# One wide transpose for the maxima, one norm for two at the input, wider cleans, range clears and new priorities in a planned transformer kernel

## What is computed

```python
x = x + LN(L0_attn(LN(x)))   # own input norm with gain and shift, plus positions; 6 layers of
                             # windowed attention (16 heads of 8, past 125 keys, one zero row ahead)
                             # and a GELU feed-forward of 512, post-norm
x = x + LN(L0_ffn(LN(x)))    # token shift, sigmoid gate times squared relu
x = x + LN(L1_attn(LN(x)))   # causal attention with a phase gate for each head and key
x = x + LN(L1_ffn(LN(x)))    # a router picks 3 of 8 experts for each sequence
```

## Time and profile before

| what | value |
|---|---|
| median of 3 runs | 1100.56 us (1100.5 to 1101.69) |
| span of the profiled execution, first to last instruction | 1102.7 us |
| TensorE busy (matmuls) | 994.2 us, 90% of the span |
| VectorE, ScalarE, GpSimd busy | 809.7, 763.1, 407.5 us |
| mean granted TensorE clock | 0.972 of full |

### The profile page before, as it was taken

The page is one execution under the profiler, slowest core; times in us unless marked ns, Lnnn a source line. Parts: engine busy times, 40 slices in busy tenths (PEclk is TensorE's granted clock), DMA queues, the critical chain, the costliest instruction groups (busy, mean ns, idle before and its releaser), DMA issues.

```text
span 1102.7 us, 47422 instructions
## 1 busy us (share of the span) xinstructions
PE 994.2 (90%) x20080; PEld 705.4 (64%) x20080; DVE 809.7 (73%) x2451; ACT 763.1 (69%) x1418; POOL 407.5 (37%) x544
## 2 busy tenths in 40 slices
PE   1679999999999999999998999998987988899993
PEld 0356777777777777777775777666664544555772
DVE  6777887777778887777777775879798979872320
ACT  7457666767777667767773777767767868688741
POOL 8711433333344433333344213444646353401311
PEclk9769999999999999999998999999999989999997
DMA  5522211222225211332224123221112020401220
GB/s 160 116 62 61 61 42 42 78 70 61 62 62 105 56 43 41 64 89 62 61 62 103 27 38 61 60 46 29 35 28 60 3 61 4 117 26 37 68 77 10
DMA packets 72627, 64.80 MB, mean 59 GB/s; under 512 B 16226, under 2 KB 66914, under 8 KB 72418
## 3 DMA queue, kind: packets, MB, share of 16 engines
q1 hardware_dynamic: 72418, 61.78, 23.3%
HBM read 15.70 MB, written 1.05 MB: 15 GB/s over the span
## 4 chain that ended last, share of the span: by engine, by line
PE 72%; DVE 11%; ACT 5%; POOL 5%; issue 3%; SPq 1%; DMA 1%; POOLq 0%; DVEq 0%; ACTq 0%
PE b L775 11%; PE b L887 9%; PE b L878 8%; PE b L676 7%; PE b L756 5%; PE b L790 4%; PE b L959 4%; PE b L949 4%; PE b L709 4%; PE b L806 2%; PE b L846 2%; PE b L871 2%; DVE mx L1218 2%; ACT probs L1021 2%; PE b L862 2%
## 5 line engine op out<-in xcount | busy, mean ns | idle before, releaser
L1021 ACT ACTIVATE probs<-b 128x443 f32<-128x443 f32 (+2 forms) x736 | 354.0, 543 | 137.5 <-PE b L756 96.5
L1218 DVE TENSOR_REDUCE mx<-b 128x2 f32<-128x378 f32 (+1 forms) x768 | 353.0, 508 | 93.9 <-PE b L709 93.5
L676 PE MATMUL b<-band,identb 64*64 64x252 bf16 x2304 | 170.4, 286 | 18.4 <-DVE mx L1218 8.1
L775 PE MATMUL b<-probs,vals 128*32 128x189 f32 (+5 forms) x3968 | 182.8, 311 | 1.2 <-DVE mx L1218 0.3
L775 PEld LDWEIGHTS b<-probs,vals 128*32 128x32 f32 x3968 | 115.1, 110 | 47.2 <-issue 12.2
L1543 POOL TENSOR_SCALAR veps<-mv 128x4 f32<-128x4 f32 x48 | 11.0, 230 | 352.4 <-DVE mv L1324 352.4
L756 PE MATMUL b<-qpack,kpack 64*64 64x189 bf16 (+5 forms) x3968 | 137.0, 236 | 0.3 <-issue 0.3
L709 PE MATMUL b<-kpack,qpack 62*64 62x189 bf16 (+1 forms) x3072 | 122.0, 239 | 1.0 <-issue 1.0
L676 PEld LDWEIGHTS b<-band,identb 64*64 64x64 bf16 x2304 | 67.0, 105 | 83.6 <-issue 36.5
L887 PE MATMUL b<-w,hid 128*128 128x128 f32 x768 | 110.1, 287 | 0.0
L1215 DVE TENSOR_REDUCE mx<-b 128x1 f32<-128x512 f32 (+7 forms) x256 | 99.3, 444 | 14.1 <-PE b L724 13.7
(11 more groups left out here) (173 smaller groups left out, 1695.7 us busy)
## 6 DMA issues: line engine op xcount, KB each, us to landing
kpack<-kparts SPq DMA_DIRECT2D x168, 128.2 KB
qpack<-qparts SPq DMA_DIRECT2D x168, 128.0 KB, 3.4
qpack<-mrows SPq DMA_DIRECT2D x224, 4.0 KB
w<-in_w SPq DMA_DIRECT2D x12, 256.0 KB, 4.3
w<-in_wa SPq DMA_DIRECT2D x12, 256.0 KB, 3.3
w<-in_wb SPq DMA_DIRECT2D x12, 256.0 KB, 3.7
rowt<-in_rowt SPq DMA_DIRECT2D x6, 384.0 KB, 3.4
stream<-in_x SPq DMA_DIRECT2D x4, 256.0 KB, 4.0
```

What stands on the lines that cost most here:

```text
L676: pe.matmul(out, identb[rows, rows], rhs.unsqueeze(1).to_broadcast([64, 2, 2, EDGE]), start=True, stop=False, skip_group_check=True)
L775: mm = pe.matmul(bank("sum", u, group)[32 * j:32 * j + 32, q0:q0 + w - skip], vals[:, u % 2, at:at + 32], probs[:, n % SETS, j, col + skip ...
L1021: act.activation(probs[:, n % SETS, j, 0:width], bank("exp", u, v, b)[:, 0:width], ACT.Exp, scale=SCALE).then_inc(a_emptied, 1)
L1218: red = dve.tensor_reduce(out[:, 2 * tb:2 * tb + 2], read[:, 0:2 * width].rearrange("p (t k) -> p t k", k=width), AX.X, ALU.max)
```

## The change

It has these parts. (1) The maxima's parts of both halves get a tile of 128 columns, cleared once, and each half is turned by one 128x128 transpose instead of two 128x32 ones; the half's 64 rows are copied. (2) The two norms at the input become one, with the root taken of variance x (1 + eps) + eps squared. (3) The cleans of `qpack` and `kpack` are written as 32-bit words. (4) The semaphores are cleared by ranges of numbers. (5) The first pack of the keys is issued from ScalarE's queue. (6) The planner gets new times for changes of shape, an account of instruction fetches on TensorE, and new values for all its worths and biases (the two long tables, left out here).

```diff
-TURN = {"q": 195, "k": 195, "out": 195, "hid": 195, "ffn": 195, "mixin": 195, "mixv": 195, "ehid": 195, "eout": 195,
-        "cat": 150, "turn": 150, "norm": 150, "rows": 150, "weigh": 140, "v": 250}
-TURN_LEAST, TABLE_LOAD = 95, 1400
-TURN_WORTH = 15422
-TABLE_WORTH = 195519
-SLACK = {"act": 346, "dve": 0, "pe": 89, "pool": 2020, "sp": 1379}
...
+TURN = {"q": 200, "k": 200, "out": 205, "hid": 200, "ffn": 200, "mixin": 200, "mixv": 200, "ehid": 200, "eout": 200,
+        "cat": 152, "turn": 152, "norm": 152, "rows": 152, "weigh": 165, "v": 200, "phase": 200}
+TURN_LEAST, TABLE_LOAD = 122, 1400
+FETCH, FETCHED, VLOADS = 3850, 256, 80
+TURN_WORTH = 827
+TABLE_WORTH = 188731
+SLACK = {"act": 323, "dve": 0, "pe": 23, "pool": 472, "sp": 953}
...
 CAP = {"exp": 3, "heads": 8, "hid": 3, "max": 8}
+
+
+def fetched(name):
+
+    kind, c = name[0], len(name) > 1 and isinstance(name[1], int) and causal(name[1])
+    if kind == "max":
+        return 16 * len(CAUSAL_TILES[name[3]]) if c else 24
+    if kind == "score":
+        return 16 * len(CAUSAL_BANKS[name[3]]) if c else 40
+    if kind == "weigh":
+        return 16 * len((CAUSAL_BANKS if c else CHUNK_BANKS)[name[3]])
+    if kind == "v":
+        return VLOADS - 16 * c
+    return {"q": 4, "k": 4, "phase": VLOADS - 16, "parts": 8, "turn": 8, "cat": 8, "out": 16, "norm": 8, "hid": 4, "ffn": 16,
+            "rows": 8, "mixin": 20, "mixv": 16, "router": 4, "logits": 4, "spread": 4, "ehid": 4, "eout": 16}[kind]
...
         clock = {e: 0 for e in self.order}
+        count, arrives = 0, 0
         mode = {e: None for e in self.order}
...
             job.start, job.end = at, at + job.cost
+            if e == "pe":
+                n = fetched(name)
+                ahead = FETCHED - count % FETCHED
+                if n >= ahead:
+                    crossed = max(at + job.cost * ahead // n, arrives)
+                    job.end = crossed + job.cost - job.cost * ahead // n
+                    arrives = crossed + FETCH
+                count += n
             clock[e] = job.end
...
         add("pool", ("lower", which, u), 1734, [("rest", which, u)], line="lower" + which)
-        add("sp", ("pack", which, u), 3700,
+        first = which == "k" and u == 0
+        add("act" if first else "sp", ("pack", which, u), 3900,
             [("lower", which, u), ("score", u - BUFS, PAIRS // 2 - 1, banks_of(u - BUFS) - 1) if u >= BUFS
-             else (which + "clean", u)], line="pack", landing=2500)
+             else (which + "clean", u)], line=None if first else "pack", landing=2500)
     if c:
...
                 line="top")
-            add("pe", ("parts", u, half), 110, [("split", u, half)], takes=[("parts", u, half)], mode=STRIPE, line="parts")
+            add("pe", ("parts", u, half), 110, [("split", u, half)], takes=[("parts", u, half)], mode=WIDE, line="parts")
             add("act", ("mrows", u, half), 251,
...
-    norm_jobs(plan, b, 0, ("x", b))
-    norm_jobs(plan, b, 1, ("nscale", b, 0))
+    norm_jobs(plan, b, 1, ("x", b))
     add("dve", ("place", b), 1334, [("nscale", b, 1), ("places",)], line="place")
...
     for n in range(BUFS):
-        add("pool", ("qclean", n), 3500, line="qclean")
-        add("act", ("kclean", n), 4000, [("row",)], line="kclean")
+        add("pool", ("qclean", n), 1800, line="qclean")
+        add("act", ("kclean", n), 2050, [("row",)], line="kclean")
     add("pool", ("places",), 1230, [("in",)])
...
         def _(pool):
-            for s in semaphores:
-                pool.sem_clear(s)
+            numbers = sorted(s.num for s in semaphores)
+            first = 0
+            for i, n in enumerate(numbers):
+                if i + 1 == len(numbers) or numbers[i + 1] != n + 1:
+                    pool.sem_clear(range(numbers[first], n + 1))
+                    first = i + 1
...
         qparts, kparts = sb("qparts", [P, 3, SEQ], BF16), sb("kparts", [P, 3, HEADED], BF16)
-        qpack = sb("qpack", [P, BUFS, 1 + PAIRS * SEQ], BF16)
+        qpack = sb("qpack", [P, BUFS, 2 + PAIRS * SEQ], BF16)
         kpack = sb("kpack", [P, BUFS, PAIRS, KEYS], BF16)
...
         mx = sb("mx", [P, 2, 2, 2, 2 * TILES])
-        mparts = sb("mparts", [P, PARTS, 32], BF16)
-        mrows = sb("mrows", [32, PARTS * P], BF16)
+        mparts = sb("mparts", [P, 2, PARTS, 32], BF16)
+        mrows = sb("mrows", [P, P], BF16)
         probs = sb("probs", [P, SETS, LANES, 512])
...
         v_odd = sem("v_odd")
+        mparts_clean = sem("mparts_clean")
         negated, mparts_ready, max_loaded = sem("negated"), sem("mparts_ready"), sem("max_loaded")
...
-            return stream[:, b, :] if k in (0, 3, 5, 7) else xres[:, b, :]
+            return stream[:, b, :] if k in (1, 3, 5, 7) else xres[:, b, :]
...
                 pe.wait_ge(mparts_ready, 2 * u + half + 1)
-                for part in range(PARTS):
-                    mm = pe.transpose(out[0:32, part * P:(part + 1) * P], mparts[:, part, :], identb[:, :])
-                mm.then_inc(a_filled, 1)
+                pe.wait_ge(mparts_clean, 1)
+                pe.transpose(out[:, 0:P], mparts[:, :, :, :].rearrange("p a n c -> p (a n c)"), identb[:, :]
+                             ).then_inc(a_filled, 1)
...
                 act.wait_ge(a_filled, filled("parts", u, half))
-                act.copy(mrows[:, :], bank("parts", u, half)[:, :].bitcast(BF16)[0:32, 0:PARTS * P]
-                         ).then_inc(a_emptied, 1)
+                rows = slice(64 * half, 64 * half + 64)
+                act.copy(mrows[rows, :], bank("parts", u, half)[:, :].bitcast(BF16)[rows, 0:P]).then_inc(a_emptied, 1)
...
+            def pack_first():
+                act.wait_ge(k_clean, 1)
+                act.wait_ge(k_lo, 1)
+                for r, n in enumerate(KROLES):
+                    act.dma_start(kpack[r:P:ROLE_STEP, 0, :, 0:HEADED], kparts[:, n, :]).then_inc(k_packed, 16)
+
             def clean_keys(buf):
-                act.activation(kpack[:, buf, :, :].rearrange("p v k -> p (v k)"),
-                               zero[:, :].to_broadcast([P, PAIRS * KEYS]), ACT.Identity, bias=max_row[:, 0:1]
+                act.activation(kpack[:, buf, :, :].rearrange("p v k -> p (v k)").bitcast(F32),
+                               zero[:, :].to_broadcast([P, PAIRS * KEYS // 2]), ACT.Identity, bias=max_row[:, 0:1]
                                ).then_inc(k_clean, 1)
...
                     clean_keys(*where)
+                elif kind == "pack":
+                    pack_first()
                 elif kind == "sin":
...
                 dve.wait_ge(d_emptied, emptied("max", u, LANES * half + 3, tops_of(u) - 1))
-                dve.tensor_scalar(mparts[:, 0, :], top_, -1.0, None, ALU.mult).then_inc(negated, 1)
+                dve.tensor_scalar(mparts[:, half, 0, :], top_, -1.0, None, ALU.mult).then_inc(negated, 1)
                 dve.wait_ge(negated, n + 1)
-                dve.scalar_tensor_tensor(out=mparts[:, 1, :], in0=top_, scalar=-1.0, in1=mparts[:, 0, :],
+                dve.scalar_tensor_tensor(out=mparts[:, half, 1, :], in0=top_, scalar=-1.0, in1=mparts[:, half, 0, :],
                                          op0=ALU.mult, op1=ALU.subtract).then_inc(mparts_ready, 1)
...
                 n = plan.nth("nstats", b, k)
-                if k == 0:
+                if k == 1:
                     dve.wait_ge(x_loaded[b], 16)
-                elif k == 1:
-                    dve.wait_ge(normed_ready, plan.nth("nscale", b, 0))
                 elif k == 2:
...
             dve.memset(ones[:, :], 1.0).then_inc(half_ready, 1)
+            dve.memset(mparts[:, :, :, :], 0.0).then_inc(mparts_clean, 1)
             for kind, *where in plan.order["dve"]:
...
                 pool.wait_ge(nmv_ready, plan.nth("nstats", b, k))
-                pool.tensor_scalar(nveps[:, b, :], nmv[:, b, :, 1], EPS, None, ALU.add).then_inc(nveps_ready, 1)
+                if k == 1:
+                    pool.tensor_scalar(nveps[:, b, :], nmv[:, b, :, 1], 1 + EPS, EPS * EPS, ALU.mult, ALU.add
+                                       ).then_inc(nveps_ready, 1)
+                else:
+                    pool.tensor_scalar(nveps[:, b, :], nmv[:, b, :, 1], EPS, None, ALU.add).then_inc(nveps_ready, 1)
                 pool.tensor_scalar(nminus[:, b, :], nmv[:, b, :, 0], -1.0, None, ALU.mult).then_inc(nminus_ready, 1)
...
                 elif kind == "qclean":
-                    pool.memset(qpack[:, where[0], :], 0.0).then_inc(q_clean, 1)
+                    pool.memset(qpack[:, where[0], :].bitcast(F32), 0.0).then_inc(q_clean, 1)
...
                         sp.dma_start(qpack[BODY + part:P:64, u % BUFS, first:first + 2 * SEQ],
-                                     mrows[:, part * P + 64 * h:part * P + 64 * h + 64]).then_inc(max_loaded, 16)
+                                     mrows[64 * half + 32 * part:64 * half + 32 * part + 32, 64 * h:64 * h + 64]
+                                     ).then_inc(max_loaded, 16)
...
```

(37 more changed lines are left out.)

8 lines of the change are left out of this document (removed).

## The result

The changed kernel took 1091.71 us (median of 7 runs, 1087.81 to 1096.27), the kernel before beside it on the same chip 1101.69 (7 runs, 1099.67 to 1104.06). The ratio is 0.9903, with a 95% interval of 0.9883 to 0.9922: 1.0% faster. The forecast was 1081 us in a range of 1062 to 1095, so the direction and the range hold, but half of the forecast gain did not come (10.0 us of 19.6). The profiled execution of the changed kernel took 1091.71 us and spans 1089.9; the rest, 1.8 us, lies around the span.

The account below looks back on a forecast made before the run. TensorE, busy 90% of a 1102.7 us span, was taken to fill the body, between a waiting head and a tail. Gains 8 + 0 + 6.6 + 1 + 4 = 19.6 give 1083.1; less 2.1, 1081 us, range 1062 to 1095.

Parts of the forecast that it names:

- The head: Start of the kernel: one norm and word-wide cleans bring the first projection forward from 23.36; 8 us gained, bounds 4 to 11.
- The clears: After the last store: one or two range clears replace 91 single ones on GpSimd; 6.6 us gained, lower bound 0.
- The moved pack: First key pack moved from SyncE's queue to ScalarE's: 0, bounds 3.9 us gained and 3.8 lost.
- The wide transposes: Maxima turned by 56 single 128x128 transposes instead of pairs: 1 us gained, bounds 6 gained and 16 lost.
- loss of 3 to 5 us for an unmoved order: Maxima's 128x128 transposes left at their old places, about half beside weighs, would cost 3 to 5 us.
- The planner: New order of every queue closes a tenth of TensorE's idle time from 550 to 950: 4 us, bounds 30 gained, 20 lost.
- leave nothing there: Body to 550 us: TensorE's 8.7 idle us leave the new order nothing to gain but the number of shape visits.
- The reference: Sums made against the profiled span of 1102.7 us; the unprofiled median, 1100.56, taken as 2.1 us lower throughout.
- B: Rival: head's gain lost in later waits, transposes beside weighs cost 3; about 9.6 us gained, 1091 us; chance 0.17.
- C: Rival: smaller worth of keeping a shape adds visits at 0.29 us each; four more per unit give 1113 us; chance 0.10.
- A: Rival: order closes half the idle time from 550 to 950 and saves shape visits; 24 us more, 1057 us; chance 0.20.

Follow-up runs that it names:

- the last experiment: Changed kernel, same orders, with one DMA of the six in each pack of queries and keys (result not computed in full): 1080.22 us, ratio 0.9798.
- four edits in the old order: Kernel before with range clears, word-wide cleans, one norm and wide transposes, without new planner or moved key pack: 1091.6 us, ratio 0.9902.

## Why the prediction was right or wrong

**The head, 8 us: right.** In the order of before, one norm gave 4.6 and the cleans 2.4, 7.0 together, and in the changed kernel unit 0 is 7.1 us ahead. The first projection at 15.26 lies in the stretch given (13.6 to 15.7), but near its late end mostly for other reasons than the one given: the scaling started 1.1 us late and `place` took 0.6 us more, while the clean ahead of the copy cost about 0.2.

**The clears, 6.6 us: right.** 6.5 measured alone. That they lie inside the time was argued from 1100.56 being later than the first clear, and holds. One clear of the whole range takes 0.53 us, not about 0.1.

**The moved pack, 0: right,** with its reason: the queue was relieved, the DMA engines were not (share 1.15), and ScalarE's next copy into state came 3.6 us later.

**The wide transposes, 1 us gained: not there.** Measured, 1.0 slower in the old order with no change inside the interval, and in the new order the narrow ones are as fast. The bounds held. The prices were somewhat high: 0.11 for a transpose beside wide jobs is 0.07, and 0.29 for a visit of its own ahead of a weigh is 0.16. And a narrow pair at a weigh was not nearly free: its second transpose, at 192.83, is missing from the earlier trace rows, and the two together cost 0.07. So the loss of 3 to 5 us for an unmoved order was too high; with the measured prices gain and loss cancel.

**The planner, 4 us gained: wrong, and this is the step that failed.** It had been called a choice. The idle time from 550 to 950 that was to be filled is 40.5 us after 40.1, and the old order with the same edits is as fast. What I had not seen is in "leave nothing there": 8.7 idle us between 100 and 550 became 11.8. Most of this rise are gaps in which TensorE has no instructions: those over 0.25 us add up to 1.8 us there in the kernel before and to 4.6 in the changed one (3.2 in its second profiled execution). I named the account of fetches and put no price on what it accounts for. The trace of before had this kind of gap too, at number 8129, again a multiple of 256 away, and I passed over it:

```profile
224.91 0.30 PE L676 MATMUL b<-band,identb 64*64 64x252 bf16 x4 [1.49 <-issue]
```

**The reference, 1.1 us too low.** The prediction took the 2.1 us between profiled span and median for a fixed difference. An execution's time is 1.8 us longer than its span (1091.71 against 1089.9; 1079.25 against 1077.4 in the last experiment); the profiled execution of before was a long one, and the median of 1100.56 that was shown is at the low side of what that kernel does (1101.69 beside the result, 1101.66 to 1103.15 beside the experiments). That is 1.1 of the 10.7 us by which 1081 missed. The other 9.6 are the gain, 19.6 forecast and 10.0 found. By the experiments with one edit each the clears are 0.1 of it (6.5 measured), the head 1.0 (7.0) and the transposes 2.0 (-1.0); what remains, 6.5, lies with the planner's 4 that did not come and with 2.5 that is lost when the parts stand together. How these 2.5 divide between the new order, the sum of four measurements' noise and a real loss is not told apart.

**The rivals.** B comes nearest, 1091, but for another reason: the ends carried almost fully (13.5 us of 14.6), the order gave nothing. Its second figure, 1088 if the clears lay outside the time, was a wrong sum: without their 6.6 about 3 us would be left, 1098. C, more visits from a smaller worth of keeping a shape, is refuted as a mechanism: the number of changes of shape fell from 905 to 881, and putting the old worth back made the kernel 5% slower at the same number of changes. That C priced a real risk of the order is true all the same: three edits of the planner's account, worth and tables cost 33 to 60 us. A has nothing for it.

The best that was measured with the full computation is within the noise of the changed kernel: four edits in the old order (1091.6) or the new order with the narrow transposes (1091.3).

## What to carry to other kernels

Look first at what a kernel does before its first and after its last useful instruction: here 1% of the time lay in clears one by one and in a chain of two norms, and each could be had alone. An order that a planner makes with tuned priorities belongs to the costs with which it was tuned: changing one number may cost several per cent, so retuning is needed after each edit, and its worth is measured against the same edits in the old order, not against the old kernel. Where the busiest engine has gaps without a releaser, number its instructions: equal spacing points at their supply, and large transfers at that moment make it late.

## What the runs showed of the hardware

TensorE's instructions come in packets of 16 KB, one for 257 of its instructions on average, and its gaps without a releaser stand multiples of 256 apart. While bulk transfers hold the DMA engines (share 1.1) and small tiles use up instructions at about 75 per us, TensorE ran dry for up to 1.18 us in the changed kernel. The longest gap was in the four edits in the old order, where a weigh is cut in two:

```profile
342.48 0.83 PE L786 MATMUL b<-probs,vals 128*32 128x189 f32 x11
345.38 0.91 PE L786 MATMUL b<-probs,vals 128*32 128x189 f32 x13 [2.06 <-issue]
```

```profile
343.30:345.40 2.10, 0.04 (x5) 0.02 (x4) 1.65 (x5) 0.04 (x1) 0.97 (x3) 0.96 1.10 166
```

This gap cost more than its length. Behind it, after TensorE had stood nearly idle from 343.3 to 345.4, its granted clock is 0.50, or 1.2 GHz, for 3.4 us (last but two figure), and 12 scores that take 0.39 us at full clock take 0.64 there:

```profile
345.20:348.60 3.40, 3.22 (x53) 2.56 (x57) 0.00 (x0) 1.64 (x3) 2.63 (x3) 0.50 1.16 186
```

In the changed kernel, whose longest gap past 100 us is 1.18, the clock stays at full from 64.2 to 593.3 us. Whether the gaps also make the runs differ is not shown: with a sixth of the packs five runs lie within 4.9 us and the changed kernel's seven within 8.5, but with all packs and narrow transposes five runs lie within 4.0.

A wide range clear of semaphores takes 0.53 us against 74 ns for each single one. And casts on VectorE are slow while GpSimd clears memory: the 128x128 cast of the identity, which took 2.67 us beside the memset of qpack in the kernel before and ended at 15.01, just behind the memset's end at 14.93, takes 0.19 where no memset runs. The two rows, of the kernel before and of the changed one:

```profile
12.34 2.67 DVE L1448 CAST identb<-ident 128x128 bf16<-128x128 f32 x1 [0.39 <-DMA diff<-in_band_first]
```

```profile
16.60 0.19 DVE L1486 CAST identb<-ident 128x128 bf16<-128x128 f32 x1
```

The Trainium skill (SBUF — State Buffer, Who interferes with whom) describes this as a port pair that the two engines share under an exclusive lock. The long cast, which ends with the memset, agrees with it. Not every instruction of GpSimd holds a cast up: the short one ran inside a 128x4 operation on GpSimd that lasted from 16.07 to 17.20.
